# Expert choice by two search instructions, later seats in the last chain, expert weights requested at the last product, and second biases loaded in two parts

## What is computed

```python
# gnn: N=3125 nodes, 50000 edges, D=256, two graph convolutions
xw = h @ W
agg = segment_sum((dis[row]*ew*dis[col])[:, None] * xw[row], col) + (dis*dis)[:, None]*xw + b
h = relu(layernorm(agg)*g + be) + h_res
x = x + h
# mixture of experts: H=256, F=512, 16 experts, 2 for each token
xn = layernorm(x)
logits = xn @ gate_w + gate_b
vals, idx = top_k(logits, 2); w = softmax(vals)
out_e = relu(xn @ w1[e] + b1[e]) @ w2[e] + b2[e]
y = xn + sum(w[k] * out_{idx[k]})
x = x + layernorm(y)*gamma + beta
```

## Time and profile before

| | us |
|---|---|
| three runs | 1298.89, 1297.34, 1297.24 (median 1297.34) |
| profiled execution, its own time | 1299.26 |
| its span, first to last instruction | 1297.5 |
| last product of the second layer copied out | 984.43 |
| DVE's last work of block one (L774) | 1006.13 |
| PE's first transpose of an expert block (L1244) | 1028.99 |

### The profile page before, as it was taken

One profiled execution on the slowest core, in us unless ns is written; L12 is line 12 of the kernel. 1 busy time (PEld: TensorE's weight loads), 2 busy tenths in 40 slices (PEclk: granted clock), 3 DMA queues, 4 the chain that ended last, 5 costly groups with the idle time before them and its releaser, 6 DMA issues. The chain is left out here.

```text
span 1297.5 us, 19246 instructions
## 1 busy us (share of the span) xinstructions
PE 1110.8 (86%) x6434; PEld 952.6 (73%) x6436; DVE 776.2 (60%) x2155; ACT 281.1 (22%) x613; POOL 638.4 (49%) x628
## 2 busy tenths in 40 slices
PE   1888239999999996878899999999994299999967
PEld 1667117888888885757778888888883299999964
DVE  8999979713443432223426888888877345554536
ACT  0000063301111111111211111111111033333337
POOL 3788777777777777773000111111111255555525
PEclk9999999999999998788979999999997599999989
DMA  9998004043333313132035544444535622222236
GB/s 352 407 400 336 1 1 153 8 153 122 133 110 123 111 64 102 52 102 102 0 118 185 204 141 170 153 174 148 179 123 170 210 67 74 72 74 70 72 103 231
DMA packets 76191, 180.75 MB, mean 139 GB/s; under 512 B 28914, under 2 KB 58236, under 8 KB 66364
## 3 DMA queue, kind: packets, MB, share of 16 engines
q1 hardware_dynamic: 43016, 150.21, 32.0%
q0 software_dynamic: 19776, 15.76, 4.6%
q10 hardware_dynamic: 13300, 13.53, 3.3%
HBM read 122.12 MB, written 57.33 MB: 138 GB/s over the span
## 5 line engine op out<-in xcount | busy, mean ns | idle before, releaser
L425 POOL DMA_INDIRECT weights_by_cell<-w_cell,cell x391 | 442.7, 1132 | 142.5 <-issue 116.1
L1087 PE MATMUL ps<-x_rows,w 128*128 128x256 f32 x1300 | 304.2, 389 | 29.7 <-DMA w<-weights_by_cell 29.4
L1087 PE MATMUL ps<-w 128*128 128x256 f32 x1300 | 303.4, 385 | 1.1 <-ACT w L815 1.1
L1087 PEld LDWEIGHTS ps<-x_rows,w 128*128 128x128 f32 x1300 | 251.9, 196 | 66.3 <-DMA w<-weights_by_cell 31.8
L1087 PEld LDWEIGHTS ps<-w 128*128 128x128 f32 x1300 | 243.4, 192 | 32.6 <-ACT w L815 2.6
L477 POOL DMA_INDIRECT token_and_home_of_slot<-pair,slot_id x50 | 49.6, 991 | 357.3 <-DVE slot_id L746 349.4
L1400 DVE TENSOR_SCALAR hidt<-ps,b1t 128x128 f32<-128x128 f32 x232 | 65.3, 344 | 96.0 <-PE ps L1261 96.0
L575 DVE TENSOR_TENSOR layer<-ps,w 128x1024 bf16<-128x1024 f32 x98 | 116.0, 1218 | 1.2 <-PE ps L929 0.7
L1273 PE MATMUL ps<-w,hidt 128*128 (+1 forms) x464 | 109.8, 380 | 0.0
L1261 PEld LDWEIGHTS ps<-xt,w1s 128*128 128x128 f32 x880 | 107.0, 192 | 2.8
L1261 PE MATMUL ps<-xt,w1s 128*128 128x128 f32 x880 | 107.1, 275 | 0.0
(11 more groups left out here) (233 smaller groups left out, 1294.9 us busy)
## 6 DMA issues: line engine op xcount, KB each, us to landing
w<-weights_by_cell SPq DMA_DIRECT2D x49, 1600.0 KB, 7.2
weights_by_cell<-w SPq DMA_DIRECT2D x26, 1600.0 KB, 9.6
w<-in_L_ffn_w_dram SPq DMA_DIRECT2D x32, 512.0 KB, 8.8
weights_by_cell<-w_cell,cell POOLq DMA_INDIRECT x391
w<-in_x_dram ACTq DMA_DIRECT2D x1, 3072.0 KB
hot<-in_x_dram ACTq DMA_DIRECT2D x24, 128.0 KB, 2.1
normalised_rows<-hot ACTq DMA_DIRECT2D x24, 128.0 KB, 4.9
out_dram<-w SPq DMA_DIRECT2D x24, 128.0 KB
```

Of the source, the lines that this page charges most:

```text
L425: pool.indirect_dma_start(adj[:, :], bass.IndirectOffsetOnAxis(ap=cell[0:m, c:c + 1].bitcast(U32), axis=0), w_cell[0:m, n, half * CH + j:h ...
L1087: mm = pe.matmul(bank(k % 2, 0, D), ring[:, place_of(k), s * P:(s + 1) * P], tab[q][:, s, :], start=(s == 0), stop=(s == NT - 1))
```

## The change

The numbers of the changed code's lines are a few lower than those of the lines they replace.

- `choose`: the twelve steps that find and mark two experts become five: the eight largest logits sorted (`max`), their positions (`max_index`), a bound on the position, and one comparison that makes both one-hot rows. The two best logits are copied out beside this (`did` waits for nothing).
- `x1_rows` is written behind x2, not ahead of the statistics.
- `seat(22)` moves into finish_tile(24), behind its first two operations; `seat(23)` moves ahead of `choose(24)`.
- SP requests w1 of experts 6 to 15 when the last product is done (and the tile before the last has been read), and keeps only w1 of expert 5 and w2 of 5, 6, 12 for the end of the last tile.
- `b2b`: ACT loads the part of experts 0 to 3 at the start of block two, and the other two parts (experts 4 to 11 and 12 to 15) behind its work for block 1; DVE waits for them at block 4.
- POOL makes three constants less.

```diff
@@ load of expert weights (SP, end of block one)
                 sp.wait_ge(ov_ps, 2 * VT)
+                sp.wait_ge(agg_read, 2 * NT - 1)
+                for e in range(6, EXPERTS):
+                    load_up(sp, e)
                 sp.wait_ge(fold_ready, 2 * VT)
-                load_up(sp, 7)
                 sp.wait_ge(z_ready, 2 * NT)
-                for e in (5, 6):
-                    load_up(sp, e)
+                load_up(sp, 5)
+                for e in (5, 6, 12):
                     load_down(sp, e)
-                for e in range(8, EXPERTS):
-                    load_up(sp, e)
-                    if e == 12:
-                        load_down(sp, e)
@@ finish_tile (DVE)
                     if nxt is not None:
                         folding(nxt)
+                    if r_seat is not None:
+                        seat(r_seat)
                     dve.wait_ge(y_made, i + 1)
...
-                        dve.tensor_tensor(x1_rows[:, d, :], x1s, beta[:, :], ALU.add)
                         link(dve.bn_stats(stats[:, 1, :], x1s))
...
                         dve.tensor_scalar(x2[:, r % XRING, :], x1s, small[:, 1, 0:1], small[:, 1, 2:3], ALU.subtract, ALU.mult).then_inc(x2_ready, 1)
+                        dve.tensor_tensor(x1_rows[:, d, :], x1s, beta[:, :], ALU.add)
                         dve.wait_ge(x2_ready, r + 1)
@@ choose (DVE)
-                    for k in range(2):
-                        link(dve.tensor_reduce(best[:, k, d:d + 1], logit[:, :], AX_X, ALU.max))
-                        link(dve.tensor_scalar(cand[:, 0:EXPERTS], logit[:, :], best[:, k, d:d + 1], -float(EXPERTS), ALU.is_equal, ALU.mult))
-                        link(dve.tensor_tensor(cand[:, 0:EXPERTS], cand[:, 0:EXPERTS], eids_up[:, :], ALU.add))
-                        link(dve.tensor_reduce(which[:, k:k + 1], cand[:, :], AX_X, ALU.min))
-                        link(dve.tensor_scalar(one[:, r % 2, k, :], eids[:, :], which[:, k:k + 1], None, ALU.is_equal))
-                        if k == 0:
-                            link(dve.copy_predicated(logit[:, :], one[:, r % 2, 0, :].bitcast(I32), neg[:, :]))
+                    link(dve.max(tops[:, :], logit[:, :]))
+                    did(dve.tensor_copy(best[:, :, d], tops[:, 0:2]))
+                    link(dve.max_index(top_at[:, :], tops[:, :], logit[:, :]))
+                    link(dve.tensor_scalar(which[:, :], top_at[:, 0:2], EXPERTS - 1.0, None, ALU.min))
+                    link(dve.tensor_tensor(one[:, r % 2, :, :], eids[:, :].rearrange("p (a e) -> p a e", a=1).to_broadcast([P, 2, EXPERTS]),
+                                           which[:, :].rearrange("p (a e) -> p a e", e=1).to_broadcast([P, 2, EXPERTS]), ALU.is_equal))
@@ end of the second layer (DVE)
-                        finish_tile(q, d, i, nxt)
+                        finish_tile(q, d, i, nxt, r - 2 if r == NT - 1 else None)
...
-                        if r >= 2:
+                        if 2 <= r < NT - 1:
                             seat(r - 2)
...
+                seat(NT - 2)
                 choose(NT - 1)
-                seat(NT - 2)
                 seat(NT - 1)
@@ b2b (ACT, block two)
-                    for lo, hi in ((0, EXPERTS - TURN), (EXPERTS - TURN, EXPERTS)):
...
+                    load_b2(act, 0, FIXED, b2_in)
...
                     for b in range(usual + 2):
                         next_block(b)
+                        if b == 1:
+                            load_b2(act, FIXED, EXPERTS - TURN, b2_rest)
+                            load_b2(act, EXPERTS - TURN, EXPERTS, b2_rest)
@@ add_x (DVE, block two)
+                        if b == FIXED:
+                            dve.wait_ge(b2_rest, 32)
```

More of the change, by code:

```diff
@@ L234, in gnn @@
         eids = sb("eids", [P, EXPERTS])
-        eids_up = sb("eids_up", [P, EXPERTS])
         base = sb("base", [P, EXPERTS])
         live = sb("live", [P, 1])
-        neg = sb("neg", [P, EXPERTS])
         logit = sb("logit", [P, EXPERTS])
-        cand = sb("cand", [P, EXPERTS + 1])
+        tops = sb("tops", [P, 8])
+        top_at = sb("top_at", [P, 8], U32)
         which = sb("which", [P, 2])
@@ L458, in _ @@
                           allow_small_or_imprecise_dtypes=True).then_inc(routing, 1)
-                pool.iota(eids_up[:, :], pattern=[[1, EXPERTS]], base=EXPERTS, channel_multiplier=0,
-                          allow_small_or_imprecise_dtypes=True).then_inc(routing, 1)
                 pool.iota(base[:, :], pattern=[[REGION, EXPERTS]], base=0, channel_multiplier=0,
                           allow_small_or_imprecise_dtypes=True).then_inc(routing, 1)
-                pool.memset(neg[:, :], -3.4e38).then_inc(routing, 1)
-                pool.memset(cand[:, EXPERTS:EXPERTS + 1], EXPERTS - 1.0).then_inc(routing, 1)
                 pool.memset(before[:, 0, :], 0.0).then_inc(routing, 1)
                 pool.memset(live[:, :], 1.0).then_inc(routing, 1)
-                pool.wait_ge(routing, 11)
+                pool.wait_ge(routing, 8)
                 pool.affine_select(out=live[:, :], in_=live[:, :], compare_op=ALU.is_gt, fill=0.0, base=LAST,
@@ L673, in folding, with finish_tile @@
                     dve.tensor_tensor(fold[:, k % 2, 0:w], reach[:, 0:w], reach[:, 1:w + 1], ALU.subtract).then_inc(fold_ready, 1)
-                def finish_tile(q, d, i, nxt):
+                def finish_tile(q, d, i, nxt, r_seat=None):
                     bias, gain, shift = (vec[:, 3 * q + k, :] for k in range(3))
@@ L758, in _ @@
                         dve.wait_ge(combined, k + 1)
-                        finish_tile(q, d, i, nxt)
+                        r = i - NT
+                        finish_tile(q, d, i, nxt, r - 2 if r == NT - 1 else None)
                         nxt = None
-                        r = i - NT
                         if r == 1:
-                            dve.wait_ge(routing, 12)
-                        if r >= 2:
+                            dve.wait_ge(routing, 9)
+                        if 2 <= r < NT - 1:
                             seat(r - 2)
@@ L1150, in experts @@
             gb_in, diag_ready = sem("gb_in"), sem("diag_ready")
-            b_in, b2_in, counts, tv, table_ready, gap_ready, exp_ready = (
-                sem(n) for n in ("b_in", "b2_in", "counts", "table_chain", "table_ready", "gap_ready", "exp_ready"))
+            b_in, b2_in, b2_rest, counts, tv, table_ready, gap_ready, exp_ready = (
+                sem(n) for n in ("b_in", "b2_in", "b2_rest", "counts", "table_chain", "table_ready", "gap_ready", "exp_ready"))
             ids_in = [sem(f"ids_in{k}") for k in range(IDS)]
@@ L1307, in _, with load_b2 @@
                             block_of_rows(b, b == BLOCKS - 1)
+                def load_b2(act, lo, hi, landed):
+                    at = place_of_expert(lo) * D
+                    act.dma_start(b2b[:, at:at + (hi - lo) * D],
+                                  g["eb2"][lo:hi].rearrange("(a e) d -> a (e d)", a=1).to_broadcast([P, (hi - lo) * D])).then_inc(landed, 16)
                 @block.scalar
@@ L1312, in _ @@
                     act.dma_start(b1r[0:TURN * KF, :], g["eb1"][EXPERTS - TURN:EXPERTS].rearrange("e (c p) -> (e c) p", p=P)).then_inc(b_in, 16)
-                    for lo, hi in ((0, EXPERTS - TURN), (EXPERTS - TURN, EXPERTS)):
-                        at = place_of_expert(lo) * D
-                        act.dma_start(b2b[:, at:at + (hi - lo) * D],
-                                      g["eb2"][lo:hi].rearrange("(a e) d -> a (e d)", a=1).to_broadcast([P, (hi - lo) * D])).then_inc(b2_in, 16)
+                    load_b2(act, 0, FIXED, b2_in)
                     act.dma_start(gam[:, :], gamma.rearrange("(a d) -> a d", a=1).to_broadcast([P, D])).then_inc(gb_in, 16)
@@ L1424, in _ @@
                     relu_h(0, 0, expert(0))
-                    dve.wait_ge(b2_in, 32)
+                    dve.wait_ge(b2_in, 16)
                     for b in range(usual - 1):
```

## The result

The changed kernel took 1284.52 us (median of four, 1282.15 to 1285.25) against 1297.63 us for the kernel before: ratio 0.9894, 95% interval 0.9877 to 0.9911, 13.1 us faster. Five more executions on another chip gave 1282.53 us, ratio 0.9877 (0.9858 to 0.9896), 16.0 us faster than the kernel before on that chip. The profiled execution took 1282.15 us with a span of 1280.4; against the profiled one of before that is 17.1 us less.

The account below looks back on a forecast made before the run. DVE narrowly paced the second layer; then a chain of small steps and draining weights held PE until 1028.99 us. PE's start moving to 1011.2 gave 1297.34 - 17.8 = 1279.5 us, range 1276 to 1284.5.

Parts of the forecast that it names:

- rival B: Gap before block two's first transpose: SP's backlog, slow slot writes or delayed gathers hold the start; 1282 to 1287 us, chance 0.19.
- parts 1 and 2: Second layer: choose falls from 3.15 to 1.82 us, PE sets the pace at 12.89; saves 4.4 us plus 0.6.
- Tile 24: Start of the last tile: forecast at 981.2 us, 7.2 earlier than 988.44, with DVE's tile needing 11.7 us.
- part 3: Last tile: L774 at 996.3 us, 9.8 earlier; last slot write issued at 997.1, 11.8 earlier; block two at 997.4.
- part 4: SP's queue of weight loads: SP free at about 994.8 us, before POOL's 997.1, so no cost.
- 2.3 us of cover: End of block one: the margin by which SP was to be free (994.8) before POOL's last slot write (997.1).
- part 5: Drain of weight loads: 8.25 MB landed by 1006 us, lists at 1007.4, PE's start at 1011.2 against 1028.99, 17.8 us.
- part 6: Rest of the second biases in block two: landed by 1026 us, needed at 1034.5, covered by 8 us; cost zero.
- The clock: First transposes of block two: still at the low clock level (0.50) as before, so this term is zero.
- the sum: Whole kernel: 17.8 us off the span of 1297.5 and off the median of 1297.34, giving 1279.5 us.

Follow-up runs that it names:

- a_old_choose: The changed kernel with the old twelve-step search of the two experts; 1286.0 us, ratio 0.9903 to the kernel before.
- a_old_seats_2: The changed kernel with seat(22) and seat(23) back at their old places, run on a chip without the long block one; 1282.5 us, ratio 0.9884.
- a_again: The changed kernel run once more, with nothing altered, on another chip; 1282.5 us, ratio 0.9877 to the kernel before.
- a_old_b2: The changed kernel with all three parts of the second biases requested by ACT at the start of block two; 1287.2 us, ratio 0.9917.
- a_old_loads: The changed kernel with the last 14 weight loads at their old places; 1287.1 us, ratio 0.9914 to the kernel before.
- a_late4g: The changed kernel with the last four weight parts requested behind the gathers of blocks 0 and 1, remaining second biases behind block 2; 1280.0 us, ratio 0.9861.
- a_late6: The changed kernel with the last six weight parts requested behind the slot lists of blocks 0 to 3; ratio 0.9900 to the kernel before.
- b_new_choose: The kernel before with the new search alone (old places of loads, seats, biases and x1_rows); ratio 0.9956.
- a_old_seats: The changed kernel with seat(22) and seat(23) at their old places, on the chip with the long block one; ratio 0.9872.

## Why the prediction was right, point by point

The forecast was 1279.5 us, the range 1276.0 to 1284.5 and the direction faster by 18; the median came out at 1284.52, at the very edge of the range. That it isn't plainly outside is luck, for single executions scatter by 5 us. The median also lies in the band of rival B (1282 to 1287), but none of B's three mechanisms took place: SP was done at 996.8, the last slot write landed 8.4 us behind its issue, and PE waited for no gather behind block 1.

**Pace of the layer (parts 1 and 2): right to 0.1 us.** Forecast 12.89 us for 20 periods and 12.46 for the last, last product 270.25 us behind k = 30: measured 270.27. `choose` at 1.82: 1.85 for choose(22), 1.6 for choose(23). That it was DVE's tile that set the pace was read from the table of waits, not from PE's busy share; the share alone said the opposite. What the text missed is that `x1_rows` behind x2 shortens DVE's tile by 0.12 too; it changed no number, since PE was the limit anyway, but it made the expectation for a_old_choose wrong (8 for 3.5).

On the search the Trainium skill (VectorE: DVE Perf Modes, "Two Vector instructions with no wait between them") lists a value load and the search as two instructions. By that rule, the trace agrees: MATCH_VALUE_LOAD 0.08 us and FIND_INDEX8 0.17 stand there as two. The first costs one short step of 0.07, not the 0.2 of the estimate.

**Tile 24: the right time by luck.** Forecast 981.2, measured 981.25. But the changed kernel's profile was 0.8 us ahead at k = 30 already (708.38 for 709.18), so behind k = 30 the tile came 0.8 us later than forecast. DVE's tile ahead of it took 12.24 us (969.01 to 981.25), not 11.7. DVE waited 1.38 us for ACT's mark in it, where it waited 0.77 in the same tile of the kernel before:

```profile
971.86 0.45 DVE L680 COPY_PREDICATED layer<-mark,zeros 128x256 f32<-128x256 int32 x1 [1.38 <-ACT mark L849]
```

**The last tile (part 3): right within 0.8 us.** L774's successor at 995.86 (996.3), last slot write at 997.02 (997.1), block two at 997.40 (997.4); behind k = 30 each is 0.4 to 0.8 us late. But the part of these 11.8 us that the seats bring is worth nothing here: a_old_seats_2 shows that an earlier slot write gains nothing while the drain ends later.

**SP (part 4): right in its verdict, thin in its cover.** SP's last issue ended at 994.34 + 2.44 = 996.8, not at 994.8; POOL was only 0.2 us later. The 2.3 us of cover were nearly gone.

**The drain (part 5): mechanism right, size 2.5 us off, 3.3 behind the last product.** Weights were to land at 1006, 26.6 us behind the last product, and did at 1008.5, 29.85 behind it. The term that was mis-sized is the length of the drain: 8.25 MB were taken over a rate between 301 and 350 GB/s, and the mean was 279. The rate of rows 1 did hold for 27.35 us (300 GB/s, windows above); the end of the drain was missed, 2.5 us in which only 47 GB/s moved and the DMA engines were busy a quarter of the time. In a_again the last 2.4 us moved 36 GB/s. What holds the last bytes up isn't shown. So the lists needed 3.4 us and not 1.9, the gather began at 1009.6 for 1008.25, PE at 1012.67 for 1011.2. The slot write landed at 1005.4 (1005.5).

**The biases (part 6): right.** DVE waited for nothing at block 4, and the rest of the biases was in at 1021.7 (1026). a_old_b2 shows that the split is worth 3.2 us of S, less than the 5.2 that the bytes came to.

**The clock: a small term that was put at zero.** PE's first products of block two ran 1014.92 to 1020.5, 5.57 us for 32 records, where they took 5.04 before. Windows at their start, of before and then of the changed kernel:

```profile
1031.00:1033.00 2.00, 2.00 (x11) 2.00 (x10) 0.00 (x0) 0.38 (x1) 1.56 (x2) 0.50 0.41 98
1033.00:1035.00 2.00, 2.00 (x16) 2.00 (x15) 0.43 (x2) 0.00 (x0) 0.34 (x1) 0.77 0.35 107
```

```profile
1014.70:1016.70 2.00, 2.00 (x11) 2.00 (x11) 0.00 (x0) 0.38 (x1) 1.69 (x2) 0.50 0.53 156
1016.70:1018.70 2.00, 2.00 (x11) 2.00 (x11) 0.02 (x1) 0.00 (x0) 0.24 (x1) 0.50 0.99 401
1018.70:1020.70 2.00, 2.00 (x19) 2.00 (x18) 1.30 (x5) 0.00 (x0) 0.00 (x0) 0.99 0.98 387
```

The granted clock went from 0.50 (1.2 GHz) to 1.00 (2.4 GHz) some 3 us behind the first product before, and 3.8 us behind it now. Loss 0.5 us. In the other kernels these 32 records took between 5.0 and 6.35 us.

**From the profile to the median.** The profiled pair differs by 17.1 us, close to the 17.8 of the sum: 16.3 at PE's first transpose (of which 0.8 came in ahead of k = 30) and 0.8 behind it. For neither of these two 0.8 was a cause found, and neither was forecast; in S, which leaves both out, the change is worth 15.5 us and not 17.8. The missing 2.3 are the drain's. The medians differ by 13.1. The profiled execution of before, 1299.26, lay 1.6 us above its median, that of the changed kernel 2.4 below its own. The rest, 17.1 to 13.1, lies in the last step of the sum: the difference of two executions was set on a median, with a scatter of 5 us from execution to execution that the three runs shown, 1.7 us apart, did not tell of. In the second set of executions the medians are 16.0 us apart. What scatters was not found.

## What to carry to other kernels

Before a short chain is made shorter, list what else must have arrived at its end. Here, in the changed kernel, the slot lists were issued 3 us ahead of the end of the drain: slot writes 3.7 us later (a_old_choose) or 1.7 us later (a_old_seats_2) cost 0.3 us or less in the gap, while a drain that ended 5.0 us later (a_old_loads) cost 4.7. An engine with 99.5% busy time may still be the one that waits; the count of waits and the period of a repeated row say who sets the pace. In this kernel bulk loads were best requested as early as their memory was free (a_old_loads shows the price of the later place), or, for those needed last, so late that the small transfers on the way to the next stage were through (a_late4g). Issued behind the lists but ahead of the gathers, as in a_late6, they met the gathers.

## What the runs showed of the hardware

- The first gather of block two began 1.0 to 1.1 us behind the landing of the last weight load in before, changed, a_again, a_old_loads, a_old_b2, a_old_seats_2 and b_new_choose, whichever queue the rest of the traffic was on; where the weights were in earlier, it began 2.5 to 3.2 us behind the issue of the list.
- 1.57 MB on ACT's queue held SP's last load back by 3.3 us.
- The bound on the positions (L719, two elements, uint32 in) took 0.40 to 0.42 us in the 22 tiles in which an indirect DMA of POOL ran beside it, and 0.17 in the three in which none did; so it was in all nine profiled kernels with the new search. Beside the row at 980.17 above stands POOL's:

```profile
979.64 0.97 POOL L470 DMA_INDIRECT token_and_home_of_slot<-pair,slot_id  x1 [10.22 <-DVE slot_id L739]
```

  Its neighbours in `choose` show no such difference. That POOL is the cause isn't shown, since no run moved one of the two.
- On one chip the copy of the first product stood at 636 to 651 us instead of 260, with DVE, ACT and PE idle for releasers that the profile doesn't show, while the stretch S of the same kernel was 2.0 us shorter there (a_old_seats, a_old_seats_2). The cause is open; it is why S and ratios, and not the times, were compared there.
